# Two-layer attention and experts on one core: the experts' chunk loop written out, and the first chunk's routing placed in the attention's last 16 tiles

## The reference

```
x = x + attention(layernorm(x), ctx, ctx)      # 16 heads of 8, causal mask, softmax, Wq for q, k and v, Wo
x = x + experts(layernorm(x))                  # below
x = x + autocorrelation(layernorm(x), ctx)     # by FFT, the 4 best delays
x = x + ternary(x)                             # layer norm, quantised weights, one matmul

experts(x): shared = silu(x Ws_up) Ws_down
            aff = x centroids^T;  idx = the 8 largest of aff + bias
            w = sigmoid(aff[idx]);  w = w / (sum(w) + 1e-8);  cw = w scattered to 64 experts
            h = silu(x W_up[e]);  y = h W_down[e];  shared + sum over e of cw[e] * y[e]
```

## Time and profile before

| | us |
|---|---|
| median of three runs | 1292.41 (1291.2 to 1294.64) |
| the profiled execution, its own time | 1289.56 |
| its span, first to last instruction | 1287.8 |
| start of VectorE's last add of the attention | 311.88 |
| start of the experts' first instruction | 320.86 |

### The profile page before, as it was taken

The page is one execution under the profiler, slowest core; times in us unless marked ns, Lnnn a source line. Parts: engine busy times, 40 slices in busy tenths (PEclk is TensorE's granted clock), DMA queues, the critical chain, the costliest instruction groups (busy, mean ns, idle before and its releaser), DMA issues. The chain is left out here.

```text
span 1287.8 us, 29796 instructions
## 1 busy us (share of the span) xinstructions
PE 1238.5 (96%) x9113; PEld 997.9 (77%) x9113; DVE 1067.4 (83%) x2062; ACT 922.9 (72%) x1525; POOL 770.2 (60%) x828
## 2 busy tenths in 40 slices
PE   6999999996999999999999999999999999899986
PEld 4777777774788888788878878788888888799976
DVE  5878888886788879879889889879889887689986
ACT  4778888884777777676777777777777776777761
POOL 3765665662556556656657556656657533477773
PEclk9999999998999999999999999999999999999988
DMA  5401101100976776876876877876777777111004
GB/s 127 111 27 32 30 29 31 30 20 5 218 179 167 184 181 154 194 169 152 195 168 168 194 171 164 194 170 163 183 172 178 182 183 181 34 34 30 22 2 131
DMA packets 126149, 159.56 MB, mean 124 GB/s; under 512 B 20840, under 2 KB 59504, under 8 KB 126064
## 3 DMA queue, kind: packets, MB, share of 16 engines
q1 hardware_dynamic: 120750, 156.06, 50.3%
q10 hardware_dynamic: 5314, 2.53, 0.7%
HBM read 152.25 MB, written 6.29 MB: 123 GB/s over the span
## 5 line engine op out<-in xcount | busy, mean ns | idle before, releaser
L1036 DVE TENSOR_TENSOR e_m<-e_pu,raw 128x1024 f32<-128x1024 f32 x256 | 309.7, 1211 | 93.2 <-ACT e_pu L1099 67.7
L1099 ACT ACTIVATE e_pu<-e_pu 128x1024 f32<-128x1024 f32 x256 | 258.6, 1010 | 161.8 <-PE e_pu L1135 160.4
L1109 ACT CAST e_mh<-e_m 128x1024 fp32r<-128x1024 f32 x256 | 267.9, 1047 | 44.7 <-DVE e_m L1036 40.3
L955 POOL TENSOR_TENSOR e_ml<-e_m,e_mh 128x1024 fp32r<-128x1024 f32 x80 | 193.1, 2417 | 125.1 <-ACT e_mh L1109 124.9
L1041 DVE TENSOR_TENSOR e_ml<-e_m,e_mh 128x1024 fp32r<-128x1024 f32 x176 | 238.7, 1356 | 21.6 <-ACT e_mh L1109 20.6
L1133 PE MATMUL e_pu<-r_xh,wuh 128*128 128x512 f32 x528 | 215.0, 407 | 1.9 <-PEq L208 1.9
L1144 PE MATMUL e_py<-e_mh,wdh 128*128 128x512 f32 x528 | 208.5, 395 | 2.1 <-ACT held L1086 2.1
L1135 PE MATMUL e_pu<-r_xl,wuh 128*128 128x512 f32 x528 | 209.4, 397 | 0.0
L1134 PE MATMUL e_pu<-r_xh,wul 128*128 128x512 f32 x528 | 209.3, 396 | 0.0
L1145 PE MATMUL e_py<-e_mh,wdl 128*128 128x512 f32 x528 | 209.0, 396 | 0.0
L1148 PE MATMUL e_py<-e_ml,wdh 128*128 128x512 f32 x528 | 168.2, 397 | 1.1 <-DVE e_ml L1041 0.6
(11 more groups left out here) (231 smaller groups left out, 2360.6 us busy)
## 6 DMA issues: line engine op xcount, KB each, us to landing
raw<-gates_scratch SPq DMA_DIRECT2D x512, 256.0 KB, 4.3
x_res<-in_x_dram SPq DMA_DIRECT2D x64, 64.0 KB, 1.8
xcT<-in_ctxT_dram SPq DMA_DIRECT2D x64, 64.0 KB, 1.9
held<-in_ctx_dram SPq DMA_DIRECT2D x32, 128.0 KB, 2.2
raw<-in_L_ffn_W_up_dram SPq DMA_DIRECT2D x4, 512.0 KB, 4.4
raw<-in_L_ffn_W_down_dram SPq DMA_DIRECT2D x4, 512.0 KB, 6.0
gates_scratch<-raw SPq DMA_DIRECT2D x16, 128.0 KB, 2.3
out_dram<-t_res SPq DMA_DIRECT2D x8, 256.0 KB, 2.9
```

What stands on the lines that cost most here:

```text
L955: nc.gpsimd.tensor_tensor(flat(ml[k][:]), flat(m[k][:]), flat(mh[k][:]).bitcast(F32), ALU.subtract).then_inc(m_low[1], 1)
L1036: nc.vector.tensor_tensor(flat(m[r % 3][:]), flat(pu[r % 3][:]), flat(gt[i % SPREAD]), ALU.mult).then_inc(gated, 1)
L1099: nc.scalar.activation(flat(pu[k][:]), flat(pu[k][:]), ACT.Silu).then_inc(silued, 1)
L1109: nc.scalar.copy(flat(mh[k][:]), flat(m[k][:])).then_inc(m_high, 1)
```

## The change

In the attention the pipeline now loops only up to step 47; steps 48 to 79 are written out. The split of the weights is done in eight rounds instead of twelve, in pieces of 528 columns. Chunk 0 is routed in steps 48 to 65: its four tiles are transposed two at a time in steps 49 and 50 (beside tiles 48 and 49, with the projection waiting for the copies), the affinities come in step 51, GpSimd's parts in steps 52 to 63, VectorE's in 53 to 62, the transpose of the gates and the copy in step 65. SyncE stores the gates, waits for the store and issues the first four groups' spreads inside the attention's block. ScalarE runs one small silu after its last copy. In the experts all 16 chunks are written out. Cut to its core:

```diff
-def pipeline(eng, count, lag, unroll, step):
+def pipeline(eng, count, lag, unroll, step, looped=None):
...
-    with eng.Fori(first // unroll, count // unroll) as g:
+    looped = count if looped is None else looped
+    with eng.Fori(first // unroll, looped // unroll) as g:
...
-    for t in range(count, count + lag):
+    for t in range(looped, count + lag):
...
-    pieces = n_tiles // 4 - peeled // 4
+    looped = n_tiles - 16
+    pieces = looped // 4 - peeled // 4
...
                 routing.store(sp, 0, 0)
+                sp.wait_ge(routing.stored, 16)
+                for i in range(routing.SPREAD):
+                    routing.spread_gates(sp, 0, i)
...
+                def route(t, r):
+                    if not isinstance(t, int):
+                        return
+                    if t == looped + 5:
+                        routing.top_of(dve, 0)
+                    if t == looped + 6:
+                        routing.mark(dve, 0, (0, 1))
+                    if t == looped + 7:
+                        routing.mark(dve, 0, (2, 3))
+                    if t == looped + 8:
+                        routing.compare(dve, 0)
+                    if looped + 9 <= t < looped + 13:
+                        routing.invert(dve, 0, t - (looped + 9))
+                    if t == looped + 14:
+                        routing.add_up(dve, 0)
+                        routing.add_eps(dve, 0)
+                        routing.normalise(dve, 0)
...
-                         (add_out, 5), (row_max, 2))
+                         (add_out, 5), (route, 0), (row_max, 2))
...
-                    if isinstance(t, int) and t == n_tiles + 3:
-                        routing.ends(dve, nc.vector, "dve", 0)
-                        routing.fourth_powers(dve, nc.vector, "dve", 0)
-                        routing.denominator(dve, nc.vector, "dve", 0)
-                    if isinstance(t, int) and t == n_tiles + 4:
-                        for j in range(4):
-                            routing.invert(dve, 0, j)
-                        routing.top_of(dve, 0)
-                        routing.mark(dve, 0, (0, 1, 2, 3))
-                        routing.compare(dve, 0)
...
-                routing.weights(dve, nc.vector, "dve", 0)
-                routing.add_up(dve, 0)
-                routing.add_eps(dve, 0)
-                routing.normalise(dve, 0)
-                routing.gates_of(dve, nc.vector, "dve", 0)
...
+                    if isinstance(t, int) and t == looped + 4:
+                        routing.ends(pool, nc.gpsimd, "pool", 0)
+                    if isinstance(t, int) and t == looped + 5:
+                        routing.fourth_powers(pool, nc.gpsimd, "pool", 0, (0,))
+                    if isinstance(t, int) and t == looped + 6:
+                        routing.fourth_powers(pool, nc.gpsimd, "pool", 0, (1,))
+                    if isinstance(t, int) and t == looped + 7:
+                        routing.denominator(pool, nc.gpsimd, "pool", 0)
+                    if isinstance(t, int) and t == looped + 8:
+                        routing.low_part(pool, 0, 0)
+                    if isinstance(t, int) and t == looped + 13:
+                        routing.weights(pool, nc.gpsimd, "pool", 0)
+                    if isinstance(t, int) and t == looped + 15:
+                        routing.gates_of(pool, nc.gpsimd, "pool", 0)
...
                     nc.scalar.copy(xcT[:, r % 4, 0, :], pt_in).then_inc(turned_out, 1)
+                    if isinstance(t, int) and t == looped:
+                        act.wait_ge(raw_read, looped // 2 - peeled // 2)
+                    if isinstance(t, int) and looped <= t < looped + 2:
+                        routing.pair_out(pj, t - looped)
+                    if isinstance(t, int) and t == looped + 2:
+                        routing.affinities_out(act, pj_aff, 0)
...
+                    if isinstance(t, int) and t == n_tiles + 1:
+                        routing.gates_copy(act, pj, 0)
+                    if isinstance(t, int) and t == n_tiles + 4:
+                        act.wait_ge(preset_dve, 1)
+                        nc.scalar.activation(warm[:], cst["mhalf"][:], ACT.Silu)
...
+                    if isinstance(t, int) and looped <= t < looped + 2:
+                        routing.turn_pair(pj, t - looped)
+                    if isinstance(t, int) and t == looped + 2:
+                        routing.affinities(pe, pj_aff, 0)
                     nc.tensor.transpose(pt_in, xn[:, r % 2, :], cst["ident"][:]).then_inc(turned, 1)
...
+                    if isinstance(t, int) and looped <= t < looped + 3:
+                        pe.wait_ge((routing.half_out, routing.turned_out, routing.aff_out)[t - looped], 1)
                     nc.tensor.matmul(pj[:, 0:2, :], cst["Wq"][:], xcT[:, r % 4], start=True, stop=True)
...
+                    if isinstance(t, int) and t == n_tiles + 1:
+                        pe.wait_ge(v_out, n_tiles)
+                        routing.turn_gates(pe, pj, 0)
...
+    def turn_pair(self, pt, k):
+        for j in range(2):
+            ins = self.nc.tensor.transpose(pt[:, j, :], self.norms.xn[:, 2 * k + j, :], self.cst["ident"][:])
+        if k == 1:
+            ins.then_inc(self.turned, 1)
+
+    def pair_out(self, pt, k):
+        self.nc.scalar.copy(self.xs[:, 2 * k:2 * k + 2, :], pt[:, 0:2, :])
+        ins = self.nc.scalar.copy(self.xh[:, 0, 256 * k:256 * k + 256], pt[:, 0:2, :].rearrange("p j t -> p (j t)"))
+        ins.then_inc((self.half_out, self.turned_out)[k], 1)
...
-        def drive(eng, step):
+        def drive(step):
...
-            for n in range(GROUPS):
-                step(n, n, lambda lag, n=n: (n - lag) // GROUPS)
-            with eng.Fori(0, looped // 3) as g:
-                for r in range(3 * GROUPS):
-                    step(g * (3 * GROUPS) + (GROUPS + r), GROUPS + r, lambda lag, g=g, r=r: g * 3 + (1 + (r - lag) // GROUPS))
-            for n in range((1 + looped) * GROUPS, turns + RING):
+            for n in range(turns + RING):
                 step(n, n % (3 * GROUPS), lambda lag, n=n: (n - lag) // GROUPS)
...
+                    if isinstance(n, int) and n < SPREAD:
+                        return
```

More of the change, by code:

```diff
@@ L242, in _ @@
                 }
-                pipeline(sp, n_tiles, peeled, 4, step)
+                pipeline(sp, n_tiles, peeled, 4, step, looped)
                 sp.wait_ge(raw_landed, 16 * 10)
@@ L446, in _ @@
                 bias_parts = {8: bias_high, 9: bias_rest, 10: bias_middle, 11: bias_add, 13: bias_low}
-                pipeline(pool, n_tiles, peeled, 4, step)
-                routing.low_part(pool, 0, 0)
+                pipeline(pool, n_tiles, peeled, 4, step, looped)
                 routing.await_turned(pool, 0)
@@ L613, in step @@
                     turn(t, r)
-                pipeline(pe, n_tiles, peeled, 4, step)
-                routing.turn_gates(pe, pj, 0)
+                    if isinstance(t, int) and t == n_tiles + 1:
+                        pe.wait_ge(v_out, n_tiles)
+                        routing.turn_gates(pe, pj, 0)
+                pipeline(pe, n_tiles, peeled, 4, step, looped)
 class ChunkNorm:
@@ L696, in __init__ @@
         self.cwF = carve([4, P])[0:E]
-        self.gt = [carve([2, 512]) for k in range(4)]
+        self.gt = [carve([2, 512]) for k in range(self.SPREAD)]
         assert taken[0] <= 2 * PAIRS * P
@@ L718, in __init__ @@
         self.stored = sem("r_stored")
+        self.spread = [sem(f"r_spread{k}") for k in range(self.SPREAD)]
         self.idle = {e: sem(f"r_idle_{e}") for e in ("dve", "act", "pool", "sp", "pe")}
@@ L760, in ends, with fourth_powers @@
         ops.tensor_scalar(self.uv[:, 1], self.th, -1.0, 1.0, ALU.mult, ALU.add).then_inc(self.powers, 1)
-    def fourth_powers(self, eng, ops, name, c):
-        for k in range(2):
+    def fourth_powers(self, eng, ops, name, c, times=(0, 1)):
+        for k in times:
             wait_apart(eng, self.powers, 3 * c + 1 + k, self.idle[name])
@@ L829, in gates_copy, with spread_gates @@
         self.nc.scalar.copy(self.cwF, pt[0:E]).then_inc(self.g_out, 1)
+    def spread_gates(self, sp, b, i):
+        rows = self.scratch[b, 4 * i:4 * i + 4].rearrange("(j e) t -> e j t", e=2)
+        for e in range(2):
+            sp.dma_start(self.gt[i % self.SPREAD][64 * e:64 * e + 64], rows[e].unsqueeze(0).to_broadcast([FH, 2, 512])).then_inc(
+                self.spread[i % self.SPREAD], 16)
     def store(self, sp, c, b):
@@ L846, in experts @@
     turns = chunks * GROUPS
-    looped = (chunks - 4) // 3 * 3
     RING = 3
-    SPREAD = 4
+    SPREAD = routing.SPREAD
     with ExitStack() as mem:
@@ L882, in experts @@
         idle = {e: sem(f"e_idle_{e}") for e in ("dve", "act", "pool", "sp", "pe")}
-        spread = [sem(f"e_spread{k}") for k in range(SPREAD)]
         low_by_pool = (4, 5, 7, 10, 14, 16)
@@ L991, in step @@
                     wait_apart(sp, gated, c * FULL + (i + 1 - SPREAD), idle["sp"])
```

(7 more changed lines are left out.)

39 lines of the change are left out of this document (15 added, 24 removed).

## The result

The changed kernel takes 1278.46 us (median of four runs, 1276.8 to 1279.25) against 1292.36 (1291.2 to 1294.64) for the kernel before on the same chip: a ratio of 0.9889, with a 95% interval of 0.9871 to 0.9906. I had said 1281.0, with a range of 1275.5 to 1287.0. The profiled execution took 1278.78 where that of before took 1289.56; its span is 10.8 us shorter.

What follows compares the result with a forecast made beforehand. Bounds: TensorE in the experts, a serial chain at the seam, a one-score-buffer ring in the attention. Terms summed to -11.5 us, taking the profiled 1289.56 to 1278.1; adding the median's 2.85 gave 1281.0, range 1275.5 to 1287.

Steps and rivals of the forecast that it cites:

- (a): Attention tiles 48 to 63 written out: a tile goes from 4.40 to 4.24 us over 15 periods, -2.4 us.
- (b): ScalarE's 24 casts of 352 columns become 16 of 528, ahead of the copy TensorE's projection awaits: +2.0 us.
- (c): First chunk's transposes and affinities in attention steps 49 to 51, the projection waiting for ScalarE's copies: +2.6 us.
- (d): VectorE's routing in attention steps 53 to 62: compare beside GpSimd +1.0, small operations of step 62 +0.3, together +1.3 us.
- (e): GpSimd's routing moved into the attention's steps, covered by its waits for input: 0, at most 1 us.
- (f): Seam between attention and experts: with routing gone, experts start at 311.5 instead of 320.87, -9.4 us.
- (g): First expert chunk, with spread buffers full and table loaded; low clock for 5.46 us expected again: -0.8 us.
- (h): Experts' loop written out: 4.1 us go with the jumps, half of four chunks' short overruns 0.7: -4.8 us.
- 1, a low clock for 17 us: TensorE's clock at 0.50 for 17.07 us from the experts' start: +5.8 us, giving 1286.8; chance 0.10.
- 2, twice the price in the attention: Moved routing costs the attention twice as much, VectorE and GpSimd holding each other up: +4.5, 1285.5 us; chance 0.13.
- 3, almost free: Routing almost free in the attention and the clock never falls at the seam: 1273.7 us; chance 0.10.
- 4, holes in straight code: Experts' straight code meets unfetched instructions, a hole in each of 12 chunks costing 18 us: 1299; chance 0.03.

Runs made afterwards that it cites:

- tiles_straight: Kernel before with experts and the attention's last 16 tiles written out, casts of 528 columns, routing left at the seam: 1287.28 us, ratio 0.9957.
- experts_straight: Kernel before with only the experts' 16 chunks written out: 1284.64 us, ratio 0.9935.
- split_casts: Changed kernel with 33 casts of 256 columns, one in each step from 15 to 47, instead of 16 of 528: 1275.98 us, ratio 0.9876.
- routing_after_norm: Changed kernel with even casts, deferred second copies, no early silu, and GpSimd's routing in steps 52 to 56 waiting for VectorE's norm: 1273.61 us, ratio 0.986.
- no_warm: Changed kernel without the one-column silu that loads the table early: 1277.54 us, ratio 0.9889.
- late_spread: Changed kernel with the first chunk's spreads issued by the experts' code, not in the attention's block: 1277.74 us, ratio 0.9894.
- one_long_round: Changed kernel with chunks 1 to 12 in a loop of a single round, register waits and idle increments kept, no backward jump: 1278.96 us, ratio 0.9894.
- experts_looped: Changed kernel with the experts' loop put back (chunks 1 to 12 in four rounds): 1294.48 us, ratio 1.0004.

## Why the prediction was right

The sum said -11.5 for the profiled execution and it was -10.8; by its own steps:

(a) Written-out tiles, -2.4. Measured -1.5 (tiles_straight against experts_straight). The step that failed is the price of a written-out tile: I took 4.24 from the earlier trace rows, a tile among the first, when GpSimd and the DMAs do other work, and the later ones take 4.29; 15 periods at 0.10 are what was measured.

(b) Wider casts, +2.0. Measured +2.2 to +2.3. The cast takes 0.63 us, not 0.67; 0.15 more than before, 16 times, is 2.4, so nearly all of it is paid. split_casts shows that it need not be.

(c) Turn and affinities, +2.6. The periods from tile 46 to 49 sum to 15.86 against 12.94 in tiles_straight: +2.9, in the places named, 0.8, 0.7 and 1.4 us. None grew by the 2 us that would have made me wrong.

(d) VectorE's routing, +1.3. Measured +0.8, but not where I put it. I blamed the compare, which took 2.31 at the median in the experts; it took 0.41. The norm paid: 1.15 and 1.38 us where it takes 0.34, beside GpSimd's fourth power and low part (0.83 us in a third step, whose period did not grow). The mechanism, two engines holding each other up, was right, the victim wrong; routing_after_norm turned it around, and then the compare did pay (1.47). The Trainium skill (GPSIMD Engine Reference, Key points) says that GpSimd shares its SBUF interfaces with VectorE and contends with instructions of two SBUF inputs or in a two-port mode. The compare, with two SBUF inputs, agrees. The norm has one and two scalars a partition, so it agrees only if it ran in a two-port mode, and that no row says. The shift, which has PSUM for one input, takes its usual 1.21 us while GpSimd makes three additions with two SBUF inputs each. Timeline of the changed kernel:

```profile
301.55 1.28 POOL L414 TENSOR_TENSOR x_res<-x_res,boe 128x128 f32<-128x128 f32 x3
301.57 1.21 DVE L278 TENSOR_TENSOR prob<-ps,mx 128x1024 f32<-128x1024 f32 x1
```

Of the rest of (d): the small operations of step 62, for which I set 0.3, cost nothing: that period is 4.29. The wait for scores shrank only from 42.6 to 38.6 us (GpSimd's wait for the keys' input first, then VectorE's for scores):

```profile
POOL kx L386 <- ACT qkT L507: 75.0, 56, 2.8
DVE mx L273 <- PE ps L557: 38.6, 58, 2.8
```

(e) GpSimd, 0: it held. Its wait for the keys' input fell from 78.6 us to 75.0. In tiles_straight, which differs from the changed kernel in the attention by the routing alone, it is 82.2, so 7.2 us of waiting took in the moved work. What GpSimd's work did cost, it cost through VectorE's norm, in (d).

(f) The seam, -9.4. Measured -10.2. The chain was as described. From tile 63's shift to the experts I had 10.35 us and it was 9.58: tile 63's add was done 8.6 us behind the shift and not 9.1, and the first matmul followed the silu's end (315.64) by 0.3 us where I had 0.65 from the store's issue. The store went out 1.25 us ahead of that shift, where I had 1.15, and the first spread 2.33 later, where I had 2.3. As for the drain that the Trainium skill (ScalarE: Activation LUTs, What ACT_TABLE_LOAD costs) adds to a switch, the trace decides against it here: the copy before the load ends at 314.13, the load runs from 314.14 to 315.42, and the activation starts at 315.44.

(g) Chunk 0, -0.8. Measured -0.5: the clock stayed at 0.50 for 6.1 us of dense work and not 5.46. That is 0.1 us beyond the 6 that I had named as a sign of being wrong; at half clock the 0.65 us over 5.46 cost 0.3 us.

```profile
315.22:322.05 6.83, 6.11 (x17) 4.88 (x18) 1.23 (x1) 2.41 (x5) 1.10 (x1) 0.50 0.46 98
```

In no_warm and late_spread, where it rose earlier (4.5 and 4.1 us into the experts), chunk 0 took 46.6.

(h) The loop, -4.8. Measured -5.6: I had half of the 0.3 us extras of four chunks go, and all went. They are gone in one_long_round too, so register arithmetic does not bring them; but one of them, chunk 13, was straight code before as well, and chunk 3 of experts_looped has one ahead of any jump. What brings them stays open. The Trainium skill (Runtime: NRT & Kernel Launch, Instruction fetch mechanics) says that a taken branch out of the pages at hand forces a fetch and that straight code hides its own. Both halves agree with the runs, though no row shows a fetch: 16 straight chunks without one wait for issue at the gate, and jumps that cost 5.3 to 6.7 us on VectorE. Which jump stalls did not follow from counting instructions.

From the sum to the median: I added the 2.85 us by which the median of before lay above its profiled execution. The changed kernel's median lies 0.3 below its profiled one, so 1278.5 came out and not 1281.0. That step assumed that both kernels vary alike. The kernel before ranged over 5.3 us in 15 runs, experts_looped over 6.5 in ten, experts_straight and one_long_round over 1.4 and 0.7 in four. That jumps make the time vary is likely from these, but split_casts, without a jump, ranged over 5.1 in four, so it is not shown.

The rivals. 1, a low clock for 17 us, did not come: 6.83. 2, twice the price in the attention: 5.9 us in all against my 5.9. 3, almost free: no. 4, holes in straight code: none. That the sum came within 0.7 us is in part luck: the steps missed by up to 0.9 us with both signs, and 0.8 us slower is the start, which the change does not touch. What I had not listed is that with the loop kept, the routing's move would have been worth nothing.

## What to carry to other kernels

Price a loop's backward jump by the engine that stands still behind it, and look again after any edit to the surrounding code: the same loop cost 5.6 us in one kernel and 15.6 in the other (7.9 and 16.0 by the medians). When small work is moved into the slack of a pipelined stage, look for what GpSimd and VectorE then run at the same moment rather than at its own length, and cut long pieces in two: with 33 short casts the tiles took as long as with the 24 of before, with 16 long ones 2.2 us more. What is off the chain by a few us (an early table load, early spreads) may be left undone.

## What the hardware showed that I had not expected

- ScalarE stood still for 5.2 to 6.0 us at the same jump that cost it 0.24 to 0.27 us in the kernel before, with its own loop body unchanged.
- After each such hole in experts_looped the granted clock of TensorE fell to 0.50 for 3.41 us, so that 1.9 to 2.7 us of idle time became 4.0 to 4.8 us of lost time.
- A norm of 128 by 128 on VectorE took 0.34 us alone and 1.38 beside GpSimd's subtraction of 1.27; the compare took 0.41 alone and 1.47 beside one of 1.29. VectorE's instruction ended 0.1 to 0.3 us after GpSimd's, as if it had to wait it out. In these cases the two started within 0.1 us of each other; a looped norm into which a subtraction of 1.32 us started 0.2 us late (114.85 in the changed kernel) took its usual 0.35.
- Register waits and idle increments of 12 unrolled chunks cost no measurable time; 128 plain increments at the start of VectorE and ScalarE delayed tile 13 by 9.8 us.
